# Flamingo-style block stack on one core: the order of TensorE's turns in the heads stage

## The reference, cut to what matters

```
def _L1_xattn_ref(x, context, w_qkv, w_proj, b_proj):
    NUM_HEADS = 16
    B, N, C = x.shape
    scale = D ** (-0.5)
    qkv = (x @ w_qkv.T).reshape(B, N, 3, H, D).transpose(2, 0, 3, 1, 4)
    k = jnp.concatenate([extra_k, k], axis=2)
    v = jnp.concatenate([extra_v, v], axis=2)
    attn = jnp.einsum('bhnd,bhmd->bhnm', q * scale, k).astype(jnp.float32)
    attn = jax.nn.softmax(attn, axis=-1).astype(dtype)
    out = jnp.einsum('bhnm,bhmd->bhnd', attn, v)
    out = out.transpose(0, 2, 1, 3).reshape(B, N, C)
    return out @ w_proj.T + b_proj
...
x = x + jnp.tanh(g_xattn[1]) * _L1_xattn_ref(_layernorm(x, axis=-1), ctx_2048, ...)
```

## Time and profile before

| | us |
|---|---|
| median of 3 runs | 991.04 (989.42 to 992.75) |
| span of the profiled execution | 988.2 |
| TensorE busy | 786.9 (80%) |
| VectorE busy | 638.1 (65%) |
| ScalarE busy | 404.5 (41%) |
| GpSimd busy | 367.4 (37%) |

### The profile page before, as it was taken

The page is one execution under the profiler, slowest core; times in us unless marked ns, Lnnn a source line. Parts: engine busy times, 40 slices in busy tenths (PEclk is TensorE's granted clock), DMA queues, the critical chain, the costliest instruction groups (busy, mean ns, idle before and its releaser), DMA issues. The chain is left out here.

```text
span 988.2 us, 14913 instructions
## 1 busy us (share of the span) xinstructions
PE 786.9 (80%) x5059; PEld 537.8 (54%) x5059; DVE 638.1 (65%) x1818; ACT 404.5 (41%) x887; POOL 367.4 (37%) x512
## 2 busy tenths in 40 slices
PE   3636999745898889977989899987979879877474
PEld 1624888533444444433459666666534466766363
DVE  4773322357888888736977769998277438995421
ACT  2122444233666666761441564443300137665210
POOL 6234434177655545006844201101201005554353
PEclk9856999967999999998999899998799889998597
DMA  8605777200000000000000000000000060001210
GB/s 207 242 10 148 216 204 222 69 22 16 9 10 12 12 2 2 1 2 0 0 1 1 1 1 1 1 1 1 1 0 0 1 170 1 22 22 43 81 55 27
DMA packets 51773, 45.47 MB, mean 46 GB/s; under 512 B 6804, under 2 KB 47655, under 8 KB 51442
## 3 DMA queue, kind: packets, MB, share of 16 engines
q1 hardware_dynamic: 48146, 36.91, 12.6%
q0 software_dynamic: 3552, 7.61, 3.0%
HBM read 36.90 MB, written 7.80 MB: 45 GB/s over the span
## 5 line engine op out<-in xcount | busy, mean ns | idle before, releaser
L1712 DVE TENSOR_REDUCE scratch<-psum 128x2 f32<-128x512 f32 (+1 forms) x160 | 106.5, 685 | 38.9 <-PE psum L1419 20.2
L1630 ACT ACTIVATE scratch<-psum 128x512 f32<-128x512 f32 x160 | 94.4, 602 | 65.8 <-PE psum L1439 63.4
L237 POOL TENSOR_SCALAR veps<-moments 128x4 f32<-128x4 f32 (+1 forms) x48 | 10.0, 209 | 282.1 <-DVE moments L158 280.3
L935 DVE SCALAR_TENSOR_TENSOR scratch<-psum,b_block_bias,scratch 128x256 f32<-128x256 f32 (+1 forms) x48 | 18.6, 430 | 73.7 <-ACT scratch L1090 68.0
L1009 POOL DMA_INDIRECT scratch<-pair_rows,b_gather_at x39 | 39.2, 1006 | 70.3 <-PE psum L1138 44.5
L2513 PE MATMUL psum<-late,scratch 128*128 128x512 f32 x128 | 57.0, 606 | 5.7 <-DVE routing_wide L2456 5.0
L2722 POOL TENSOR_TENSOR scratch<-scratch,arena 128x1024 f32<-128x1024 f32 x16 | 30.6, 1912 | 71.5 <-DVE arena L2961 71.5
L303 PE MATMUL psum<-ident,XN 128*128 128x128 f32 x144 | 29.7, 340 | 33.8 <-DVE XN L169 27.8
L1439 PE MATMUL psum<-scratch,arena 128*128 128x256 bf16 x256 | 49.2, 274 | 5.4 <-ACT scratch L1610 4.4
L1419 PE MATMUL psum<-arena 128*128 128x512 bf16 x128 | 49.6, 393 | 1.5 <-DVE scratch L1712 1.5
L240 POOL TENSOR_TENSOR rstd<-veps,minus_half 128x4 f32<-128x4 f32 (+1 forms) x48 | 47.9, 997 | 6.6 <-POOL veps L237 0.2
(11 more groups left out here) (463 smaller groups left out, 2073.6 us busy)
## 6 DMA issues: line engine op xcount, KB each, us to landing
arena<-in_L_ffn_w SPq DMA_DIRECT2D x72, 128.0 KB
arena<-in_L_ffn_wg SPq DMA_DIRECT2D x24, 256.0 KB
wide<-in_L_xattn_Wkv SPq DMA_DIRECT2D x1, 2048.0 KB
wide<-in_L_ffn_W SPq DMA_DIRECT2D x1, 2048.0 KB, 8.8
late<-in_L_ffn_W SPq DMA_DIRECT2D x8, 256.0 KB, 6.5
pair_results<-scratch SPq DMA_DIRECT2D x15, 128.0 KB
X<-in_x SPq DMA_DIRECT2D x2, 512.0 KB, 5.0
C<-in_ctx SPq DMA_DIRECT2D x2, 512.0 KB, 6.5
```

What stands on the lines that cost most here:

```text
L1630: a.activation(out, bank[3 + e % 2][:, :], ACT.Exp).then_inc(s["exp"], 1)
L1712: v.tensor_reduce(out, bank[m % 3][:, :].rearrange("p (h t) -> p h t", t=n), AX.X, ALU.max, negate=True).then_inc(s["maxed"], 1)
```

## The change

Four places of the stage's hand-written order change, on TensorE at steps 1 and 11 the order of two blocks, and three engines take the work on the divided heads one step later: TensorE's turn from step 5 to 6 and its output product from 7 to 8, ScalarE's copy from 6 to 7, VectorE's add from 8 to 9. No instruction is added or taken away.

```
@@ TensorE, extras
             if at == 1:
+                if ahead:
+                    if not first:
+                        t.wait_ge(s["masked"], 4 * b + 4)
+                    project(b + 1, 7)
                 if late:
                     t.wait_ge(s["masked"], min(4 * b + 2, 4 * B))
                     turns.wait_halves(t, min(b + 2, 2 * NG))
                     turn_parts(b - 2, 1)
-                if ahead:
-                    if not first:
-                        t.wait_ge(s["masked"], 4 * b + 4)
-                    project(b + 1, 7)
...
-            if at == 5 and late:
+            if at == 6 and late:
                 if ahead:
                     t.wait_ge(s["split"], 3 * (b + 1) + 3)
                 turn_out(b - 2)
-            if at == 7 and late:
+            if at == 8 and late:
                 project_out(b - 2)
...
             if at == 11:
+                if ahead:
+                    t.wait_ge(s["q_turned"], 2 * (b + 1) + 1)
+                    turn_keys(b + 1, 0, 7)
                 if behind:
                     if late:
                         t.wait_ge(s["added"], 2 * (b - 2) + 2)
                     turn_parts(b - 1, 0)
-                if ahead:
-                    t.wait_ge(s["q_turned"], 2 * (b + 1) + 1)
-                    turn_keys(b + 1, 0, 7)
@@ ScalarE, extras
-            if at == 6 and late:
+            if at == 7 and late:
                 copy_out(b - 2)
@@ VectorE, extras
-            if at == 8 and late:
+            if at == 9 and late:
                 add(b - 2)
```

## The result

The median of 22 runs is 993.81 us, against 990.86 us for 22 runs of the kernel before on the same chips. The ratio is 1.0031 with a 95% interval of 1.0017 to 1.0044, that is 1.7 to 4.4 us slower. The forecast was 994.8 us. One of the 22 runs took 1213.98 us, with TensorE's mean granted clock at 0.635 where the others have 0.894 to 0.910; it is left out of the ratio, and without it the median is 993.61 us.

A forecast was written before the change was run, and what follows sets the result against it. TensorE leads from step 1 to 9, and VectorE is full from step 9 to the next step 1. Per round +0.61 us, times 5, plus 0.33 and 0.34, gives 3.72 us: 991.04 becomes 994.8 us, range 991.4 to 996.8.

The forecast's parts named there:

- Step 1: TensorE, projection ahead of the turn of parts: starts when ScalarE's mask L1604 ends, gaining 0.25 us of a 1.14 us stop.
- The turn of the divided heads: TensorE, steps 5 and 6: L1480 leaves the wait for ScalarE's copy L1610 and costs +0.34 us a round.
- The output product: TensorE, steps 7 and 8: same block one step later between like neighbours, input ready, TensorE's sum unchanged.
- The add: VectorE, steps 8 and 9: the L1739 pair moves from a wait into the full stretch, +0.60 us a round.
- the third rival: VectorE's add waits for GpSimd at its new place, 0.53 us a round more, 997.4 us; chance 9%.
- Step 11: TensorE, keys ahead of parts: the 0.73 us stop stays, its cause changing from ScalarE to VectorE's L1696; cost 0.
- Step 16: TensorE's key-major product: its wait for a ScalarE copy is covered because TensorE is late, -0.08 us a round.
- The sum: Rounds 2 to 6: +0.61 us each, 3.05; with +0.33 and +0.34 for rounds 6 and 7, 3.72 us in total.
- The entry of round 6: Mask ends after the copy there, so the projection starts later: loses 0.08 instead of gaining 0.25 us, +0.33.
- Round 7: No next batch: VectorE's add is free, but the turn still leaves the wait for L1610, +0.34 us.

The follow-up runs named there:

- Experiment 2: Kernel before with only the swap at step 11 (turn of keys ahead of turn of parts): 989.97 us, ratio 0.9985.
- experiment 10: Changed kernel run again unaltered: 993.29 us, one run; its timed runs form a lower group (990.6 to 995.7 us) and an upper group (998 to 1000 us).
- experiment 4: Changed kernel with VectorE's add back at step 8, ahead of the maxima of step 9: 997.36 us, ratio 1.0051.
- experiment 5: Kernel before plus an unread 128x512 memset on VectorE at step 8, behind the add: 999.81 us, one run.
- experiment 7: Kernel before with VectorE's copy of queries at step 8 instead of 9: 990.01 us, one run.
- experiment 9: Kernel before with the divided heads' turn, copy and product one step later, add left at step 8, no swaps: 996.53 us, one run.
- experiment 8: Kernel before with swaps at steps 1 and 11, copy of queries at step 8, their turn ahead of step 8's value sums: 989.58 us, ratio 1.0009.
- experiment 1: Kernel before with only the swap at step 1 (projection ahead of turn of parts): 990.29 us, ratio 0.9996.

## Why the prediction was right

The kernel is slower, for the reason given, and the sum was too large: 3.72 us for a measured 2.65 in the stage. That the time came out only 1.0 us under the forecast is in part luck.

- **Step 1.** Predicted -0.25 a round with ScalarE's L1604 as releaser and a stop of about 0.9 us; measured 0.89 us, the right releaser, and from the mask's end to the score of step 2 1.64 us before (298.98 - 297.34) and 297.95 - 296.50 = 1.45 now: -0.19. Counting both blocks at their old lengths missed 0.06: the projection, now first behind a stop, takes 0.96 us to the next start and not 0.87.
- **The turn of the divided heads.** It left the wait for L1610, as predicted, and costs. But from the product of step 6 to L1462 it took 305.91 - 305.10 = 0.81 us before and takes 305.05 - 304.07 = 0.98 now: +0.17 for a predicted +0.34. This is the term that was mis-sized. From the product to L1480 is 0.23 us (304.07 to 304.30), not the 0.33 taken from L1462's rows, and from it to the next start 0.22, not 0.27. The first price was read at a neighbour with another tile shape, the second at L1480 itself, but where it stood behind a stop.
- **The output product.** Predicted 0; from L1462 of step 7 to the score of step 9 TensorE takes 308.15 - 305.05 = 3.10 us, and 309.01 - 305.91 = 3.10 before.
- **The add.** Predicted +0.60, the main term; measured +0.53. The pair, followed at once by the copy, takes 309.18 to 309.70, 0.52 us: the 0.60 was the length of the group, the next instruction starts 0.08 before its end. L1739 itself kept its price (340 to 352 ns over all sixteen in the changed trace, 341 to 351 before), so the third rival is out, and the rule of the Trainium skill (SBUF — State Buffer, section SBUF: two separate sides), by which an add with only one input in SBUF does not take the shared port, fits (of its two tensors only X lies there, besides the gate, one number per partition): at 309.18, where the pair starts, GpSimd is in its own cast L1252 (309.04 to 309.44).
- **Step 11.** Predicted 0 with L1696 as new releaser: so it is, with the stop at 0.58 us for 0.73. Experiment 2 shows that the missing wait would only have moved to step 14.
- **Step 16.** Predicted -0.08; the product starts 0.23 us after its score instead of 0.30.
- **The sum.** -0.19 + 0.17 + 0.53 - 0.08 = +0.43 a round against +0.61; the trace has 27.40 - 26.98 = +0.42. The entry of round 6 went as predicted: the projection there waits for L1604, and of the 2.49 us lost from round 1 to the start of round 7 (405.71 - 243.33 against 404.52 - 244.63) the five rounds' 5 x 0.42 = 2.10 leave 0.39, for a predicted 0.33. Round 7 cost 22.44 - 22.28 = 0.16 us (L1474 of round 7 to that of round 8) for a predicted 0.34, the turn's error again. The stage came out at +2.65 for a predicted 3.72. The timed +3.0 us lies between the two, with an interval of 1.7 to 4.4 that holds both. It is above the stage's value with the help of five runs of the changed kernel that fell into the upper group of experiment 10: the other sixteen have a median of 992.9 us, 2.2 over the 990.7 of before without its one such run. The prediction had no term for this, and in the time it hides part of the turn's error.

## What to carry to other kernels

A stop says only that something else is late. Before filling one, read what the filler itself waits for, and then which engine has no idle time between there and the end of the round: 0.66 us on VectorE cost 0.57 behind its last wait, while a swap that removed 0.55 us of a TensorE stop brought 0.07. Work that lies under a wait costs nothing until it is moved out of it, so price the place that it goes to and not the stop that it came from. And where parts of a microsecond are at stake, compare one stretch of the trace: whole runs of one and the same kernel lay 6 us apart for a cause outside the stage.

## What the runs showed of the hardware that was not expected

**A small cast that sometimes takes twice as long.** VectorE's casts of 128x16 from f32 to bf16, from SBUF to SBUF (L1687, L1690, L1692), mostly take 0.19 to 0.24 us. In experiments 4, 5, 7 and 9 eleven of them take 0.43 to 0.49 us. All eleven start 0.64 to 0.70 us after GpSimd starts an indirect DMA (L1031). GpSimd's row in experiment 9, with the cast at 310.76:

```profile
310.11 1.13 POOL L1031 DMA_INDIRECT arena<-pair_results,b_slot_bits  x1 [0.17 <-issue]
```

In no profile does a cast that starts up to 0.62 us after such an issue, or 0.89 to 1.3 us after it, take over 0.24 us. Apart from these eleven, only casts L1687 of the first two rounds are longer: 0.25 to 0.27 us in seven profiles, 0.38 in experiment 7, 0.39 and 0.30 in experiment 8, each beside a cast or memset of GpSimd (L1252, L1319). Moving VectorE's work by a quarter of a microsecond can so cost 0.28 us more, or not: in experiment 7 the slow cast is L1692, and it costs nothing, since the maxima behind it start 0.09 us after its start (310.60 to 310.69), as they start 0.08 us after it in the kernel before (312.96 to 313.04). No experiment took the DMA away, so the link is one of time alone; it is not shown that GpSimd holds something that the cast needs.

**The price of an f32 block depends on what is ahead of it.** The projection takes 0.87 us to the next start behind L1474 and 0.96 or 0.97 us behind a stop: 296.55 to 297.51 in the changed kernel, 296.71 to 297.68 in experiment 1. What stands behind it is not the cause: in round 1 of the kernel before it follows a stop and has a score product behind it, as in the earlier trace rows, and takes 0.97 us (244.63 to 245.60). Why it does was not tried.
